# Self-attention stages: another layout of the stored query and key parts, another place of the value projection

## The reference

```python
# L1_attn (fifth block; apply_rope rotates pairs of features of q and k)
q, k = apply_rope(q), apply_rope(k)
scores = jnp.einsum('bhqd,bhkd->bhqk', q * (1.0 / jnp.sqrt(jnp.float32(hd))), k)
out = jnp.einsum('bhqk,bhkd->bhqd', jax.nn.softmax(scores, axis=-1), v)
# L1_ffn (sixth block; no rotation)
scores = jnp.einsum('bqhd,bkhd->bhqk', q, k) / jnp.sqrt(jnp.float32(Dh))
ctx = jnp.einsum('bhqk,bkhd->bqhd', jax.nn.softmax(scores, axis=-1), v)
```

## Time and profile before

| | us |
|---|---|
| median of 3 runs | 1984.81 |
| the profiled execution | 1984.79 |
| its span, first to last instruction | 1983.0 |
| TensorE busy | 1692.6 |
| VectorE busy | 1329.6 |
| ScalarE busy | 1066.6 |
| GpSimd busy | 275.3 |

### The profile page before, as it was taken

How to read it: one execution, slowest core, us unless ns; L and a number is a source line. 1 busy time by engine, 2 the same in 40 slices (tenths; PEclk the granted TensorE clock), 3 DMA queues, 4 the chain that set the end, 5 groups by cost and what they waited for, 6 DMA issues and landing times.

```text
span 1983.0 us, 34606 instructions
## 1 busy us (share of the span) xinstructions
PE 1692.6 (85%) x13836; PEld 918.5 (46%) x13836; DVE 1329.6 (67%) x2148; ACT 1066.6 (54%) x1898; POOL 275.3 (14%) x248
## 2 busy tenths in 40 slices
PE   6988868999689998856999999999999768986686
PEld 4566645666557887521333333333333334552342
DVE  4233344460457999549999999999981786239556
ACT  3312122878534776211999999999998015213410
POOL 3223013898130000300000000000000000000000
PEclk9999979999788999975999999999999879986878
DMA  8124012989433665256434434434200261044100
GB/s 315 64 85 123 1 43 59 298 277 306 145 117 126 216 214 181 75 96 94 82 59 81 93 59 79 95 59 78 63 25 2 44 71 45 1 76 56 44 0 21
DMA packets 144621, 196.61 MB, mean 99 GB/s; under 512 B 34422, under 2 KB 109832, under 8 KB 140200
## 3 DMA queue, kind: packets, MB, share of 16 engines
q1 hardware_dynamic: 142732, 190.07, 37.2%
q0 software_dynamic: 1728, 4.33, 0.7%
HBM read 143.04 MB, written 51.00 MB: 98 GB/s over the span
## 4 chain that ended last, share of the span: by engine, by line
DVE 43%; PE 40%; issue 5%; DMA 4%; POOL 3%; ACT 2%; SPq 1%; another core or an unknown queue 0%; DVEq 0%; ACTq 0%; POOLq 0%
DVE mx_part L2159 27%; DVE mx L2252 3%; PE pair L1543 3%; PE bank L1182 3%; PE pair L1215 3%; DVE w_lo L1980 2%; PE pair L1137 2%; PE bank L1035 2%; PE pair L1150 2%; DMA xT<-x_slots 2%; PE bank L1318 2%; PE bank L249 2%; PE pair L1377 2%; PE bank L1079 2%; POOL k_part L2459 2%
## 5 line engine op out<-in xcount | busy, mean ns | idle before, releaser
L1709 ACT ACTIVATE pexp_all<-bank 128x512 f32<-128x512 f32 x1024 | 551.8, 596 | 98.6 <-PE bank L1332 85.0
L2159 DVE TENSOR_REDUCE mx_part<-pair 128x2 f32<-128x1024 f32 x512 | 583.1, 1216 | 17.0 <-PE pair L1304 14.8
L1318 PE MATMUL bank<-pexp_all,vst 128*17 128x256 f32 x4096 | 321.7, 386 | 6.0 <-issue 6.0
L1304 PE MATMUL pair<-kst,qs 49*128 49x512 f16 x1024 | 210.0, 407 | 44.8 <-DVE mx_part L2159 28.0
L1332 PE MATMUL bank<-qs,kst 52*128 52x256 f16 x2048 | 203.2, 271 | 0.0
L1304 PEld LDWEIGHTS pair<-kst,qs 49*128 49x128 f16 x1024 | 50.4, 93 | 273.7 <-DVE mx_part L2159 215.1
L1332 PEld LDWEIGHTS bank<-qs,kst 52*128 52x128 f16 x2048 | 120.7, 95 | 57.0 <-ACT pexp_all L1709 18.4
L1719 ACT ACTIVATE pexp_all<-bank 128x512 f32<-128x512 f32 x128 | 67.6, 595 | 122.0 <-PE bank L1440 121.9
L1318 PEld LDWEIGHTS bank<-pexp_all,vst 128*17 128x17 f32 x4096 | 68.6, 95 | 114.7 <-issue 105.2
L1215 PE MATMUL pair<-w_hi,hid_hi 128*128 128x256 f16 x368 | 102.4, 278 | 8.2 <-issue 5.0
L1654 ACT ACTIVATE hid_f<-bank,b 128x256 f32<-128x256 f32 (+1 forms) x152 | 78.6, 518 | 52.0 <-PE bank L1182 35.1
(11 more groups left out here) (313 smaller groups left out, 2979.6 us busy)
## 6 DMA issues: line engine op xcount, KB each, us to landing
w_f<-in_w_all SPq DMA_DIRECT2D x34, 1024.0 KB, 5.8
kst<-k_scr SPq DMA_DIRECT2D x192, 128.0 KB
v_scr<-v_st SPq DMA_DIRECT2D x64, 272.0 KB, 3.3
vst<-v_scr SPq DMA_DIRECT2D x16, 1088.0 KB, 5.6
ctx_sb<-in_ctx SPq DMA_DIRECT2D x16, 1024.0 KB, 4.9
cT<-in_ctxT SPq DMA_DIRECT2D x32, 512.0 KB, 5.7
k_scr<-k_part SPq DMA_DIRECT2D x128, 128.0 KB, 3.6
x_slots<-zeros SPq DMA_DIRECT2D x1, 3840.0 KB, 21.2
```

Of the source, the lines that this page charges most:

```text
L1304: last = pe.matmul(pair[n % 2][:, e * 512:(e + 1) * 512], qs[g % NBK][rws, p, qt * P:(qt + 1) * P], kst[g % NBK][rws, p, kb * 512:(kb + 1) ...
L1318: last = pe.matmul(bank[3][32 * h:32 * h + HV, 0:S], vst[g % 2][:, c, h * HV:(h + 1) * HV], unit_exp[n % NUE][:, p * S:(p + 1) * S], start ...
L1709: act.activation(unit_exp[n % NUE], bank[SCORE_BANKS[n % 3]], ACT.Exp, scale=SCALE).then_inc(s_exp, 1)
L2159: dve.tensor_reduce(mx_part[:, :, 2 * p + qt, kb], pair[n % 2][:, :].rearrange("p (e k) -> p e k", e=2), X_AXIS, ALU.max).then_inc(s_mx, 1)
```

## The change

- `self_scr` is laid out as [queries or keys, part, half, 32 features of a head pair, 8 head pairs, 512]: the two batches of a half stand side by side in a row of 512 values, and the 8 pairs behind one another, so that one feature row of a half is 8 KB in one piece.
- A store writes its 128 partitions as 4 pairs by 32 features by 512 values (1 KB each).
- A half has 8 loads instead of 12: for queries and for keys, and for e = 0 and 1, one of 32 partitions that takes both parts, and one of 16 partitions that takes the high part again.
- The pairs lie in another order in `sa.q` and `sa.k` (`stack_of`); the maxima rows of a batch are every second pair, and are stored by six DMAs instead of three.
- TensorE makes the value tiles behind the first units, one behind each: all eight in the first stage (`lead=0`), four of eight in the second (`lead=4`, four stay ahead). The wait for the last low part moves ahead with the first unit.
- ScalarE copies the values (`take_values` in its program, ahead of `self_exp`) instead of VectorE.

```diff
-        self_scr = [dram(f"self_scr{i}", [2, 2, B, D, S], F16) for i in range(2)]
+        self_scr = [dram(f"self_scr{i}", [2, 2, 2, 2 * HD, H // 2, 2 * S], F16) for i in range(2)]
-        SELF_LOADS = 12
+        SELF_LOADS = 8
-        SELF_ROWS = 3 * 16
+        SELF_ROWS = 2 * 3 * 16
+        def stack_of(b, pair_):
+            return 2 * PAIRS_B * (b // 2) + 2 * pair_ + b % 2
                     for i in range(3):
                         at = R_MAX + i
-                        sp.dma_start(sa.q[at:at + HALF + 1:HALF, PAIRS_B * b:PAIRS_B * (b + 1), :],
-                                     m_prt[32 * b:32 * b + 32, i, :]).then_inc(signals["mrow"].s, 16)
+                        for qt in range(2):
+                            dst = sa.q[at:at + HALF + 1:HALF, stack_of(b, 0):stack_of(b, PAIRS_B - 1) + 1:2, qt * P:(qt + 1) * P]
+                            sp.dma_start(dst, m_prt[32 * b + qt:32 * b + 32:2, i, :]).then_inc(signals["mrow"].s, 16)
                         for part, src in enumerate((sa.hi, sa.lo)):
-                            sp.dma_start(scr[n, part, bs, m * P:(m + 1) * P, :].rearrange("b p q -> p b q"),
-                                         src[:, half, m, n * 512:(n + 1) * 512].rearrange("p (b q) -> p b q", b=2))\
+                            sp.dma_start(scr[n, part, half, :, 4 * m:4 * m + 4, :].rearrange("f h x -> h f x"),
+                                         src[:, half, m, n * 512:(n + 1) * 512])\
                                 .then_inc(signals["fst"].s, 16)
                     for n in range(2):
-                        order, dst = (((0, 1, 0), sa.q), ((0, 0, 1), sa.k))[n]
-                        for r, part in enumerate(order):
-                            for e in range(2):
-                                src = scr[n, part, bs].rearrange("b (h e d) q -> e d (b h) q", e=2, d=HD)[e]
-                                at = HALF * e + HD * r
-                                sp.dma_start(dst[at:at + HD, 2 * PAIRS_B * half:2 * PAIRS_B * (half + 1), :], src)\
-                                    .then_inc(signals[f"qk{half}_loaded"].s, 16)
+                        both, one, dst = ((0, 2, sa.q), (1, 0, sa.k))[n]
+                        for e in range(2):
+                            fs = slice(HD * e, HD * (e + 1))
+                            at = HALF * e + HD * both
+                            sp.dma_start(dst[at:at + 2 * HD, 2 * PAIRS_B * half:2 * PAIRS_B * (half + 1), :],
+                                         scr[n, :, half, fs].rearrange("s f h x -> s f (h x)"))\
+                                .then_inc(signals[f"qk{half}_loaded"].s, 16)
+                            at = HALF * e + HD * one
+                            sp.dma_start(dst[at:at + HD, 2 * PAIRS_B * half:2 * PAIRS_B * (half + 1), :],
+                                         scr[n, 0, half, fs]).then_inc(signals[f"qk{half}_loaded"].s, 16)
                 for job in range(len(SELF_JOBS)):
                     project(job)
-                values(range(0, T))
+                values(range(sa.lead))
                 sa.wait(pe, "flo", len(SELF_JOBS))
                 for b in range(2):
                     for i in range(SELF_UNITS):
                         first_pass(b, i)
+                        if b == 0 and sa.lead + i < T:
+                            values([sa.lead + i])
+            def take_values(sa):
+                for t in range(T):
+                    sa.wait(act, "vproj", t + 1)
+                    act.activation(sa.v[:, t, :, 0:HD], bank[2 + t % 2][:, 0:D].rearrange("p (h d) -> p h d", d=HD), ACT.Copy)\
+                        .then_inc(signals["vtaken"].s, 1)
```

More of the change, by code:

```diff
@@ L576, in build, with __init__ @@
         class SelfAttention:
-            def __init__(self, turn, scope):
+            def __init__(self, turn, scope, lead):
                 i = f"self{turn}_"
-                self.turn = turn
+                self.turn, self.lead = turn, lead
                 self.hi = sb(i + "hi", [P, 2, KT, NTOK], F16, scope)
@@ L592, in build @@
         with ExitStack() as sc:
-            sa5 = SelfAttention(0, sc)
+            sa5 = SelfAttention(0, sc, lead=0)
             cosT = sb("cosT", [P, S], F32, sc)
@@ L611, in build @@
         with ExitStack() as sc:
-            sa6 = SelfAttention(1, sc)
+            sa6 = SelfAttention(1, sc, lead=4)
             b2_l = sb("b2_l", [ER, D], F32, sc)
@@ L922, in self_io @@
                 for half in range(2):
-                    bs = slice(2 * half, 2 * half + 2)
                     for i in range(4):
@@ L1404, in first_pass @@
                     for p in range(2):
-                        at = PAIRS_B * b + 2 * g4 + p
+                        at = stack_of(b, 2 * g4 + p)
                         for e in range(2):
@@ L1439, in scores @@
                     rws = head_rows(e, R_MAX + 3)
+                    b, g4 = divmod(g, H // GH)
+                    at = stack_of(b, 2 * g4 + p)
                     return pe.matmul(bank[SCORE_BANKS[(2 * n + e) % 3]][:, p * S:(p + 1) * S],
-                                     sa.k[rws, 2 * g + p, c * P:(c + 1) * P], sa.q[rws, 2 * g + p, :], start=True, stop=True)
+                                     sa.k[rws, at, c * P:(c + 1) * P], sa.q[rws, at, :], start=True, stop=True)
                 for job in range(len(SELF_JOBS)):
                     project(job)
-                values(range(0, T))
+                values(range(sa.lead))
                 sa.wait(pe, "flo", len(SELF_JOBS))
@@ L1724, in _ @@
             act_turn(act, turn4)
+            take_values(sa5)
             self_exp(sa5)
@@ L1739, in _ @@
                                bias=col(("L1_ffn_bq", "L1_ffn_bk")[n], m)).then_inc(signals["fhi"].s, 1)
+            take_values(sa6)
             self_exp(sa6)
@@ L2238, in self_attention @@
             def self_attention(sa, take_projection):
-                def take_values(tiles):
-                    for t in tiles:
-                        sa.wait(dve, "vproj", t + 1)
-                        dve.tensor_copy(sa.v[:, t, :, 0:HD], bank[2 + t % 2][:, 0:D].rearrange("p (h d) -> p h d", d=HD))\
-                            .then_inc(signals["vtaken"].s, 1)
                 ring = Ring()
@@ L2273, in self_attention @@
                     take_projection(job)
-                take_values(range(0, T))
                 for b in range(2):
```

## The result

The changed kernel took 2051.98 us in the median (2045.95 to 2054.52) against 1984.85 for the kernel before in the same session: the medians are 67.1 us apart, and the ratio of the executions is 1.0329, with a 95% interval of 1.0301 to 1.0357, which is 65 us at 1985. The forecast was +61.4 us, ratio 1.031.

What follows compares the result with a forecast made beforehand. The prediction saw a wait for half 0's stacks bounding the second self-attention, TensorE and VectorE the first. Shifts of 26.4 and 35.0 us, 61.4 together, on 1984.8 gave 2046 us; range 2005 to 2068.

Steps and rivals of the forecast that it cites:

- The mechanism: Self-attention DMAs: the smaller slowest dimension of both sides sets the engines, 2 for two-part loads, 4 for stores; chance 0.78.
- The loads: Stacks loaded back from HBM: 24.0 us per half instead of 15.4, with bounds of 22.1 and 25.4 us.
- the "one" loads: Four 16-row loads a half, on 16 engines; they add 1.3 us to the two engines of the two-part loads.
- Half 0's stores: Stores before the first loads: 1.75 us each; half 0 stored at 1582.4 and 1779.4 us in the two stages.
- Half 1's stores: Stores standing behind half 0's loads on the two engines: 14.0 us for the eight.
- The sum: Both self-attentions: 26.4 + 35.0 = 61.4 us slower, 2046 us in all.
- the shift of 26.4 and 35.0: Delay of unit (batch 2, unit 0), first reader of half 1's stacks, in us in the first and second self-attention.
- "Just in time": Half 1's stacks before the change: said to arrive just in time for unit (2, 0), at 1618.01 and 1806.44 us.
- First scores ahead of the values: First self-attention: by itself 7.3 us gained, first unit at 1591.7 instead of 1599.05; 0 here, hidden by the stacks' wait.
- Rival 1: All self-attention loads and stores run on 16 engines: 2 to 10 us faster in all, 1978 us; chance 0.13.
- ScalarE's copies: Value copies moved from VectorE, which loses 8 of 0.42 us, to idle ScalarE: effect 0, at most one copy.
- Maxima rows: Six issues on SP instead of three per batch: +1.6 us, hidden or at most 1.5 us a stage.

Runs made afterwards that it cites:

- parts_inside: Changed kernel with scratch laid out as queries or keys, half, pair, e, part, feature, so two-part loads have 32 rows on both sides and stores 8 outside: ratio 1.0020.
- loads_16_rows: Changed kernel with each half loaded by 12 one-part loads of 16 rows of 8 KB, stores left as changed: ratio 1.0064 to the kernel before.
- layout_only: Changed kernel with the old order: values ahead of all units and copied by VectorE; new layout, stores and loads kept: ratio 1.0327 to the kernel before.
- Order_only: Kernel before with values behind the first units (all eight, then four of eight) and copied by ScalarE; old layout, stores and loads: ratio 1.0041.
- pairs_outermost: Changed kernel with head pairs outside the features in the scratch: stores of 128 rows of 1 KB, 12 loads a half: ratio 1.0003 to the kernel before.
- after_again: The changed kernel, unchanged, run again on another chip for an undisturbed profile: ratio 1.0315 to the kernel before.

## Why the prediction was right, and where not

**The mechanism: right.** Dimensions of 2, 4, 8 and 16 or more outside go with 52 to 53, 85 to 94, 183 to 192 and 343 GB/s and shares of 0.13, 0.27, 0.54 and 1.15 (the last for the stores of before; the 85 is from the stores of the second stage, 1770 to 1772). Undoing the loads alone took 1.0315 to 1.0064, undoing both 1.0003, and doing the layout alone gave 1.0327. The gap that the prediction named, that no row of before showed a small dimension on the HBM side, is closed: in the two-part load the SBUF side had 32 partitions and the HBM side 2, and it ran on two engines. The Trainium skill, page "DMA: Bandwidth & Descriptors", section "Why a DMA increments its semaphore by 16 and not by 1", says that both sides count and that the lowest-numbered engines are taken. The four widths agree with the first; that half 1's stores get stuck behind the loads fits the second, but no row here names an engine.

**The loads: right in kind, too low.** 24.0 us forecast with bounds of 22.1 to 25.4; measured 26.41, 26.38, 26.55 and 26.25 (1555.01 to 1581.42, 1592.07 to 1618.45, and the second stage), outside the bounds. The failing term is the rate of the two engines at the start. At 53 GB/s, 1,048,576 B of two-part rows take 19.8 us and the rows of the "one" loads 1.2; with 2.1 fixed that is 23.1, and 3.3 are missing. While the "one" loads run beside them (the second window of the profile above) all engines together move 118 GB/s, no more than 16-row loads alone did. The bytes bear out that the two engines are slow there. From 1556.5 to 1562.5, 673 KB move (the last of these 6 us at 83 GB/s, share 0.23; then the share is 0.16, so the "one" loads are through). 524 KB of them are the "one" loads, 66 of these on the two engines. At most 149 + 66 = 215 KB then went over the two engines, where 53 GB/s would be 318: at least 103 KB, or 1.9 of the 3.3 us. The prediction counted the "one" loads only as rows on the two engines, not as traffic beside which these engines slow down. What they compete for stays open, and no run took the "one" loads away. The Trainium skill, page "SBUF — State Buffer", section "Door 1: The DMA port swizzle (why `[64,N]` ≈ `[32,N]`)", gives 104 GB/s for partitions 0 to 15 and 189 for 0 to 31. The measured 119 and 118 lie near the first, the 162 of parts_inside, with both kinds of loads and some stores, between the two; but these loads go to several groups of partitions at once, from partition 0 and from 64 on, so the cases are not the same.

**Half 0's stores: right.** In the first stage 4.76 us from the last pair to the loads (forecast 5.06, of 1.56 + 3.5), in the second 14.7 us from the first store to the loads, 1764.14 to 1778.85 (forecast 15.56). With the 1.56 us taken as fixed, a store took (14.7 - 1.56) / 8 = 1.64 us where 1.75 was taken; how the 14.7 divide between a fixed part and a rate is not shown.

**Half 1's stores: too dear.** Forecast 14.0 us behind the loads, measured 10.65 (1581.42 to 1592.07) and 10.53. The term that was mis-sized is the 1.75 us of a store. That the stores stand behind the loads holds for the two engines that load: each of them has its 32,768 B of all eight stores still to do, and at 94 / 4 = 23.5 GB/s that is 1.39 us a store, 11.2 us in all, where the prediction had 14.0. The other two of the four do part of their share beside the loads (share 0.17 from 1570 to 1572, where the loads alone show 0.13) and are through first (0.14 and 0.09 from 1588 to 1592, two engines and fewer), but that does not bring the end forward. `loads_16_rows` bears this out: with wide loads the same stores hold the next loads back until 10.07 and 9.67 us behind the first unit.

**The sum.** The loads were 2.4 us too short, twice a stage, and the stores 0.3 to 0.9 and 3.4 us too long. So the shift of 26.4 and 35.0 was met by 27.5 and 35.2: two errors of opposite sign in each stage nearly cancelled. That the total is so near is luck; the loads alone were off by a tenth and half 1's stores by a third. The prediction named the store's 1.75 us as its weakest term, and gave the loads bounds that the measured time lies outside.

**"Just in time": not so.** The prediction read unit (2, 0) of before as waiting for half 1's stacks. The earlier trace rows say that it waits for VectorE, and in the trace of before the loads' traffic ends at about 1612.4 and 1804.4, some 5.6 and 2 us before the units at 1618.01 and 1806.44. The forecast does not suffer, since it counts from the units and not from the stacks.

**First scores ahead of the values: hidden as said, priced wrongly.** In the changed kernel it makes no difference (layout_only). But the 7.3 us that it was to gain by itself are not there. The prediction let the unit start at 1591.7, when low parts are ready, "since stacks and low parts are all it needs", without asking when the stacks are: by its own numbers 1579.74 + 15.4 = 1595.1. Order_only waits 7.50 us for them, and the first unit is 3.3 us earlier, not 7.3. So the step that failed here is the start of the first unit. The cost of interleaving was seen (1.3 us for each unit at the low clock, two or three units, against 1.4 measured: 2.55 less 1.13); with the smaller gain it prevails, and alone the order is a loss of 0.41%. Rival 1 should have stood at 1985 to 1989 instead of 1978, by the 1.0003 of pairs_outermost and the 1.0020 of parts_inside; the range left it out in either case.

**ScalarE's copies: 0 as said while the stacks are late.** By themselves they are worth 0.22%, which the prediction did not price: it counted only VectorE's time and not that TensorE's third tile waits for a bank until the last rotation is done.

**Maxima rows.** Their six issues showed up as no wait ahead of the scores in any kernel; the 0 stands as far as a trace can say.

**Left open.** What slows the two engines in the first 5 us, narrow loads with stores that cost nothing (no kernel gives the stores 16 engines at unchanged addresses without the queue being held by their number), and the 2 us by which the rest of a stage varies between kernels.

## What to carry to other kernels

Before a scratch layout is changed for longer rows, write down the slowest dimension of both sides of every DMA that touches it, as it stands after merging, and count engines by the smaller; a "2 parts" or "4 pairs" put outside costs far more than rows of 8 KB bring. Cutting the transfer by hand helps only as far as the issuing queue has time for it; better is an order of the dimensions that merges with the rows. And a step that is moved ahead starts when the last of its inputs is there, so each one's arrival is to be put beside the time that is hoped for, and the work taken away from the wait needs another place that is as free.

## What was not expected of the hardware

- Row length hardly matters for loads into 16 partitions: a half took 15.4 us in runs of 512 B (second stage of before), 13.75 in runs of 1 KB and 14.25 in rows of 8 KB, from the first issue to the first unit or the end of the last load.
- A DMA whose engines are busy holds up the queue that issues it: 7.87 and 9.30 us for an issue of 0.5 us, while some thirteen of the sixteen engines stood idle (share 0.17 from 1570 to 1572). With the 16-row loads ahead of them one issue still took 5.78 us (`loads_16_rows`). That the engines' backlog is what holds the queue is my reading.
- Issuing costs by the transfer, hardly by its size: 0.45 us for a quarter of a store, 0.50 for a whole one, so four times as many kept the queue busy for 14.7 us.
- A value tile of TensorE behind a long idle wait takes 2.07 us at the low clock level instead of 1.13, and two to three of them pass before the full clock is granted (behind waits of 20.33 us in `after_again`, 7.50 in `order_only` and 5.11 in `pairs_outermost`); the same tile after a wait of 1.0 us took 1.13.
